# Pairwise products on one core: the middle third of each tile is stored from ScalarE's queue

## The reference, cut to what matters

```python
# x: (2048, 32, 64) float32, W: (64, 64) float32
i_idx, j_idx = jnp.triu_indices(32, k=1)          # 496 pairs i < j
xw = jnp.einsum('bfe,ed->bfd', x, W)
return xw[:, i_idx, :] * x[:, j_idx, :]            # (2048, 496, 64) float32
```

## Time and profile before

| | |
|---|---|
| time, median of 3 runs | 655.48 us (654.12 to 655.57) |
| the profiled execution: its time, its span | 655.77 us, 654.0 us |
| busy: VectorE, TensorE, ScalarE | 568.9, 209.3, 101.8 us |
| DMA | 277.00 MB, mean 424 GB/s |
| stores: count, KB each, us to landing | 32 of 5280 KB, 26.5; 16 of 5312 KB, 25.6 |

### The profile page before, as it was taken

The page is one execution under the profiler, slowest core; times in us unless marked ns, Lnnn a source line. Parts: engine busy times, 40 slices in busy tenths (PEclk is TensorE's granted clock), DMA queues, the critical chain, the costliest instruction groups (busy, mean ns, idle before and its releaser), DMA issues.

```text
span 654.0 us, 3858 instructions
## 1 busy us (share of the span) xinstructions
PE 209.3 (32%) x1280; PEld 157.5 (24%) x1280; DVE 568.9 (87%) x528; ACT 101.8 (16%) x385; POOL 0.7 (0%) x6
## 2 busy tenths in 40 slices
PE   5946080803407043070430704316080431400000
PEld 4734060602305032050330603214060321300000
DVE  3999999899689996899968999999999999999940
ACT  3412030302103021030210302112030211200000
POOL 0000000000000000000000000000000000000000
DMA  8999999999999999999999999999999999999994
GB/s 329 433 450 417 447 417 415 451 418 428 434 424 438 429 433 418 432 437 430 437 416 432 430 440 426 442 421 446 424 443 427 438 423 442 426 437 433 427 443 211
DMA packets 8524, 277.00 MB, mean 424 GB/s; under 512 B 1088, under 2 KB 1088, under 8 KB 1088
## 3 DMA queue, kind: packets, MB, share of 16 engines
q1 hardware_dynamic: 6912, 260.05, 92.4%
q10 hardware_dynamic: 1600, 16.81, 6.2%
HBM read 16.81 MB, written 260.05 MB: 423 GB/s over the span
## 4 chain that ended last, share of the span: by engine, by line
DMA 54%; DVE 39%; issue 2%; PE 0%; ACTq 0%; DVEq 0%; ACT 0%
DMA out_dram<-out_ring 54%; DVE out_ring L198 39%; DMA x_sb<-in_x_dram 1%; ACTq L164 0%; PE xw_bank L125 0%; PE xT_ps L115 0%; DVEq L55 0%; ACT xw_sb L160 0%; DVEq L197 0%
## 5 line engine op out<-in xcount | busy, mean ns | idle before, releaser
L198 DVE TENSOR_TENSOR out_ring<-xw_sb,x_sb 128x384 f32<-128x384 f32 (+9 forms) x528 | 568.9, 1155 | 59.5 <-DMA out_dram<-out_ring 48.2
L125 PE MATMUL xw_bank<-W_sb,xT_sb 64*128 64x64 f32 x1024 | 138.9, 429 | 347.1 <-ACT xT_sb L155 345.1
L125 PEld LDWEIGHTS xw_bank<-W_sb,xT_sb 64*128 64x128 f32 x1024 | 118.1, 320 | 385.6 <-issue 358.9
L155 ACT COPY xT_sb<-xT_ps 128x256 f32<-128x256 f32 x128 | 48.1, 376 | 383.0 <-DVE out_ring L198 339.1
L115 PE MATMUL xT_ps<-identity,x_sb 128*128 128x128 f32 x256 | 83.7, 442 | 7.4 <-DMA x_sb<-in_x_dram 7.4
L160 ACT COPY xw_sb<-xw_bank 128x128 f32<-128x128 f32 x256 | 55.6, 270 | 74.3 <-PE xw_bank L125 74.3
L115 PEld LDWEIGHTS xT_ps<-identity,x_sb 128*128 128x128 f32 x256 | 39.4, 208 | 20.4 <-DMA x_sb<-in_x_dram 7.4
L155 ACT ACT_TABLE_LOAD x1 | 1.3, 1283 | 5.1 <-issue 5.1
L93 POOL TENSOR_SCALAR_AFFINE_SELECT identity<-identity 128x128 f32<-128x128 f32 x1 | 0.3, 295 | 0.2 <-POOL identity L91 0.2
L91 POOL MEMSET identity<- 128x128 f32 x1 | 0.2, 205 | 0.3 <-POOLq L211 0.3
L211 POOL MEMSET const-bfloat16-1.0<- 128x1 bf16 x1 | 0.1, 103 | 0.0
## 6 DMA issues: line engine op xcount, KB each, us to landing
out_dram<-out_ring SPq DMA_DIRECT2D x32, 5280.0 KB, 26.5
out_dram<-out_ring SPq DMA_DIRECT2D x16, 5312.0 KB, 25.6
x_sb<-in_x_dram ACTq DMA_DIRECT2D x6, 2048.0 KB, 21.5
x_sb<-in_x_dram ACTq DMA_DIRECT2D x4, 1024.0 KB, 13.9
W_sb<-in_W_dram ACTq DMA_DIRECT2D x2, 16.0 KB, 2.0
```

The source lines that it names most:

```text
L125: last = nc.tensor.matmul(xw_ps[g % 2][odd][:, m, :], xT_sb[g % 2][rows, m, :], W_sb[rows, :], start=True, stop=True)
L155: nc.scalar.copy(xT_sb[g % 2][:], xT_ps[g % 2][:]).then_inc(xT_copied, 1)
L198: last = nc.vector.tensor_tensor(slot[:, place:place + n, :], xw_sb[t % 2][:, i:i + 1, :].to_broadcast([LANES, n, E]), x_sb[buf][:, r, j:j ...
```

## The change

The loop of SyncE skips the middle chunk. ScalarE gets a helper, `store_middle(t)`, which waits until VectorE has finished the middle chunk of tile t and issues its store from ScalarE's queue. It is called at the end of each tile's work for the tile before, and once more after the loop. Buffers, semaphores, sizes and destinations stay as they are.

```diff
+MIDDLE = 1
@@ SyncE @@
                 for c in range(CHUNKS):
-                    sp.wait_ge(chunk_ready, t * CHUNKS + c + 1)
-                    q0, q1 = CUTS[c], CUTS[c + 1]
-                    sp.dma_start(out_tiles[g, r, :, q0 * E:q1 * E],
-                                 out_ring[c][:, 0:(q1 - q0) * E]).then_inc(stored[c], 16)
+                    if c != MIDDLE:
+                        sp.wait_ge(chunk_ready, t * CHUNKS + c + 1)
+                        q0, q1 = CUTS[c], CUTS[c + 1]
+                        sp.dma_start(out_tiles[g, r, :, q0 * E:q1 * E],
+                                     out_ring[c][:, 0:(q1 - q0) * E]).then_inc(stored[c], 16)
@@ ScalarE @@
+            def store_middle(t):
+                act.wait_ge(chunk_ready, t * CHUNKS + MIDDLE + 1)
+                g, r = divmod(t, ROWS)
+                q0, q1 = CUTS[MIDDLE], CUTS[MIDDLE + 1]
+                act.dma_start(out_tiles[g, r, :, q0 * E:q1 * E],
+                              out_ring[MIDDLE][:, 0:(q1 - q0) * E]).then_inc(stored[MIDDLE], 16)
...
                 for g in range(GROUPS):
                     if g + 1 < GROUPS:
                         copy_xT(t, g + 1)
                     copy_xw(t, g)
+                if t > 0:
+                    store_middle(t - 1)
+            store_middle(TILES - 1)
```

## The result

The changed kernel takes 656.75 us in the median of 21 runs (655.08 to 659.25), the kernel before 655.39 in 21 (654.12 to 655.91). The ratio is 1.0024, with a 95% interval of 1.0018 to 1.0031: 1.4 us slower, clear of noise and still within the 0.3% that was called "the same". The profiled execution took 656.88 us, with a span of 655.1 where the one of before had 654.0.

What follows compares the result with a forecast made beforehand. The prediction took bytes over DMA rate as the limit. 655.77 + 0 (issues) + 0 (ScalarE) + 0 (mixing) + 1.0 (order of landings) = 656.8, or 656.5 us on the median's scale; range 652 to 664.

Steps and rivals of the forecast that it cites:

- the same: Whole kernel's time: a result within about 0.3%, 2.0 us, so 653.5 to 657.4 us; chance 0.56.
- The bound: Whole kernel: its end is set by bytes over DMA rate, as long as the queue never runs dry; 38.07 us a tile.
- the 25.63 us of a landing: Steady tiles: a store's time from issue to landing, read as one store queued ahead and the store itself, 12.69 us each.
- ScalarE's part: ScalarE gains 16 waits and 16 issues, 8.3 us of issuing, hidden because it stands ready 11 us early; cost 0.
- Mixing: Middle stores beside other stores in two queues: cost 0, range 0 to 12 us; as a slower rival, chance 0.15.
- The dry queue: Around the four later loads, late landings leave too little queued: 1.0 us, range 0 to 9; as slower rival, chance 0.17.
- the first rival: Middle store behind a load in ScalarE's queue: lands late, queue empties; 664.5 us, up to 668; chance 0.17.
- The bound of 2.3 us for one moment: Two buffers landing together: while VectorE fills the first, the queue is empty for 0 to 2.3 us (11.50 + 3.5 - 12.7).
- the load ahead of the middle store in ScalarE's queue: At four moments, 81.12 us and the next three loads, it was to disturb the rhythm of landings; 0 to 9 us.
- the argument that queues take turns: Loads issued at 81.12 us landed after 35.2 us, against about 18 in order of issue, so queues alternate packet by packet.
- the 3.5 us of issue and landing: Any store: issue and landing outside the moving take at most 16.2 - 12.69 = 3.5 us, taken from the first store.
- Two signs: DMA row under 9 in a slice would show an empty queue; VectorE losing over 2 us beyond 48.2 would refute the prediction.

## Why the prediction was right, and where it was not

*The bound.* Bytes over DMA rate: shown, by the late tiles at 76.13 us for two, and by VectorE cut by 3 us a tile with next to nothing gained. One reading was too simple: the 25.63 us of a landing as one store queued ahead and the store itself. A store has landed when the last of its sixteen shares has, one by each DMA engine, and the shares of the store issued at 438.68 landed from 457.09 to 464.30. The sum holds for the engine that is last; the others have up to some 7 us less queued, and so run dry first.

*ScalarE's part.* Cost 0: the middle store of tile 0 went out at 33.94 instead of 33.47, and without loads the two kernels are equal within 0.03 us, so neither the issues nor the new wait cost anything.

*Mixing.* The bound was 0 to 12 us and the value 0; measured 0.07 us. The load rows that gave the upper bound, 0.16 to 0.75 us, measured loads beside stores, not stores beside stores.

*The dry queue.* The term was 1.0 us, between 0 and 9, in the part with loads; the measured loss is 1.4 us, and no loss is left without loads. The mechanism was right: by the packets' own times the queues run dry in all six kernels with two store queues and loads, and in no other, once the stores are running, for as much as 0.1 us. The size was good by a little luck: the same mechanism gives 0.9 us with halved loads and 5.0 with the loads in SyncE's queue. The late landing of 38 us and the stop of up to 13 us at the first later loads, told in the first rival, came as 38.1 and 12.30.

Dry time and loss go together only roughly. In each profiled execution, the dry time and what it took more than the profiled one of its base: 1.2 and 0.8 us with the faster VectorE, 1.8 and 0.8 with the load behind the middle store, 1.8 and 0.9 with halved loads, 1.8 and 1.1 in the changed kernel, 4.0 and 3.5 with the third queue, 3.5 and 5.1 with the loads in SyncE's queue. The bound of 2.3 us for one moment did not hold with the third queue, where one moment had 4.0.

*Wrong in its detail:* the load ahead of the middle store in ScalarE's queue. The runs with the loads in SyncE's and in GpSimd's queue show that a load beside two queues of stores does it from any queue that was tried. In the argument that queues take turns, the 18 us "in order of issue" left out the store that was still moving at 81.12 (issued at 68.81, landed 19.9 us later); with its 7.6 us it is 25, still well under the 35.2, so the turns stand. Also the 3.5 us of issue and landing, an upper bound, were 1.2 for a store that found the queue empty (13.9 - 12.69). Two signs were badly chosen. No slice of the DMA row fell under 9, since a slice is 16.4 us long and the dry moments were under 1. And VectorE's longer waits were no sign of loss: they went from 48.2 to 56.0 us, more than the 2 us that were to speak against the prediction, yet without loads they also rise, from 27.7 to 35.5, and nothing is lost. There the waits of an engine that does not set the end cost nothing.

*What stays open:* how large the loss is in a given execution. Five of the six kernels with two queues and loads scatter by 2.5 to 5.3 us (655.08 to 659.25 in the changed kernel, 654.56 to 659.82 with a third queue); one queue, or two without loads, stay within 2. But with halved loads the scatter is 0.3 us, and why is not known. That the phase between loads and stores decides the size, and that it matters whether the engine that is last runs dry too, is argued, not shown.

## What to carry to other kernels

Where the DMA engines have no idle time, a second queue for the same stores brings no rate. Once other transfers, here the loads, come between, it takes away the order and the spacing of the landings, and a producer that refills a short ring in order needs both: two buffers that come free together are worth no more than one, and the queue may run dry while the first is filled. Look at issue-to-landing times: a store that lands in little more than its own moving time has found an empty queue.

## What was not expected of the hardware

Two queues with stores alone move the same 432 to 433 GB/s as one, and the time agrees to 0.07 us in 654.

The sixteen DMA engines do not stay level. In the kernel before, the first and the last share of a store land 1.5 us apart for the first store and 8.6 us apart for the last one.

The issue of a load can hold its engine. With the loads in SyncE's queue, its two issues of 1024 KB at 81.55 us took 5.40 us together, where ScalarE's at 81.12 had taken 1.62; SyncE's queue then held stores as well:

```profile
81.55 5.40 SPq L103 DMA_DIRECT2D x_sb<-in_x_dram  x2
```

With the load right behind the middle store, ScalarE's issue of one load took up to 3.96 us too, where the changed kernel's at 166.44 took 0.37.
